# Gathering expert tiles six ahead of the scatter instead of five in an RWKV and mixture-of-experts layer

## The reference

```python
xt = x.reshape(-1, Hv)
logits = xt @ wg
probs = jax.nn.softmax(logits, axis=-1)
idx = jnp.argmax(probs, axis=-1)
gate = jnp.take_along_axis(probs, idx[:, None], axis=1)
onehot = jax.nn.one_hot(idx, Ev, dtype=x.dtype)
expert_out = jnp.einsum('nh,eoh->neo', xt, W) + b[None, :, :]
combine = onehot * gate
out = jnp.einsum('ne,neo->no', combine, expert_out)
...
x = _layernorm(x + out, axis=-1)
```

## Time and profile before

| | |
|---|---|
| median of 3 runs | 673.41 us (673.17 to 674.12) |
| the profiled execution's own time | 673.86 us |
| its span, first to last instruction | 671.9 us |
| busy share PE / DVE / ACT / POOL | 88% / 82% / 60% / 46% |
| the first gather starts | 510.99 us |
| the turn of tile 3 starts | 527.06 us |
| the turn of tile 38 starts | 649.60 us |
| the last scatter is issued | 662.83 us |

### The profile page before, as it was taken

The page is one execution under the profiler, slowest core; times in us unless marked ns, Lnnn a source line. Parts: engine busy times, 40 slices in busy tenths (PEclk is TensorE's granted clock), DMA queues, the critical chain, the costliest instruction groups (busy, mean ns, idle before and its releaser), DMA issues. The chain is left out here.

```text
span 671.9 us, 8986 instructions
## 1 busy us (share of the span) xinstructions
PE 588.4 (88%) x2484; PEld 437.8 (65%) x2485; DVE 554.0 (82%) x866; ACT 403.5 (60%) x735; POOL 306.2 (46%) x230
## 2 busy tenths in 40 slices
PE   0676789999999999999999999999754999999992
PEld 0464666677768667668768767865554777776771
DVE  7959898998999999999999899679956666766761
ACT  3356475477567665756747647666340577777773
POOL 4744544443551552454444544247404255655641
PEclk9779898999999999999999999999855899999997
DMA  8030020031022003004103103394203566777650
GB/s 311 4 125 1 0 63 0 2 109 63 17 72 86 32 32 125 31 0 156 31 0 126 62 1 110 98 383 161 60 20 112 139 210 217 228 218 223 222 166 6
DMA packets 36562, 67.60 MB, mean 101 GB/s; under 512 B 8560, under 2 KB 8560, under 8 KB 36532
## 3 DMA queue, kind: packets, MB, share of 16 engines
q1 hardware_dynamic: 30292, 48.29, 21.8%
q0 software_dynamic: 6240, 18.94, 9.1%
HBM read 50.17 MB, written 18.88 MB: 103 GB/s over the span
## 5 line engine op out<-in xcount | busy, mean ns | idle before, releaser
L980 POOL TENSOR_TENSOR mixed<-unsplit,mixed 128x1024 fp32r<-128x1024 f32 x44 | 104.5, 2396 | 133.8 <-ACT mixed L666 133.8
L447 PE MATMUL kb<-mixed,w_kvr 128*128 128x512 f32 x384 | 99.4, 410 | 23.5 <-DVE mixed L1321 16.5
L447 PE MATMUL vb<-mixed,w_kvr 128*128 128x512 f32 x384 | 104.1, 423 | 14.4 <-DVE evn L1159 9.0
L632 PE MATMUL y_ps<-w_e_hi,xgT 128*128 x312 | 108.6, 410 | 0.0
L447 PE MATMUL rb<-mixed,w_kvr 128*128 128x512 f32 x384 | 100.6, 411 | 4.6 <-DVE ee L1173 3.6
L447 PEld LDWEIGHTS kb<-mixed,w_kvr 128*128 128x128 f32 x384 | 74.4, 197 | 42.2 <-issue 16.2
L465 PE MATMUL y_ps<-w_o,rw 128*128 128x512 f32 x224 | 100.7, 592 | 0.0
L447 PEld LDWEIGHTS vb<-mixed,w_kvr 128*128 128x128 f32 x384 | 75.7, 201 | 36.5 <-DVE evn L1159 11.8
L447 PEld LDWEIGHTS rb<-mixed,w_kvr 128*128 128x128 f32 x384 | 72.5, 191 | 26.1 <-issue 6.2
L1110 DVE SCALAR_TENSOR_TENSOR unsplit<-diff,vec,xb 128x512 f32<-128x512 f32 x96 | 74.2, 834 | 8.1 <-PE kb L447 6.2
L990 POOL TENSOR_TENSOR ee<-ee,state 128x512 f32<-128x512 f32 x32 | 35.0, 1093 | 94.3 <-DVE state L1143 93.6
(11 more groups left out here) (198 smaller groups left out, 1052.0 us busy)
## 6 DMA issues: line engine op xcount, KB each, us to landing
bias<-b_experts SPq DMA_DIRECT2D x39, 256.0 KB
w_e_raw<-w_experts SPq DMA_DIRECT2D x8, 1024.0 KB, 11.7
rows<-x SPq DMA_DIRECT2D x28, 256.0 KB, 2.6
x_rows<-rows SPq DMA_DIRECT2D x28, 256.0 KB, 2.1
xb<-xT SPq DMA_DIRECT2D x4, 1026.0 KB, 5.5
xb<-xT SPq DMA_DIRECT2D x3, 1024.0 KB, 5.2
w_raw<-w_square SPq DMA_DIRECT2D x2, 1024.0 KB, 10.0
xb<-xT SPq DMA_DIRECT2D x2, 512.0 KB, 5.0
```

The source lines that it names most:

```text
L447: mm = pe.matmul(bank, w_kvr[m][:, a, h, o:o + P], mixed[m][:, bb, h, :], start=(k == 0), stop=(k == 3 * CH - 1))
L632: mm = pe.matmul(y_ps[:, parity, :], xgT[:, third, a, c, :], w[:, bass.ds(e, 1), c, :].rearrange("p u o -> p (u o)"), start=(c == 0 and (a ...
L980: pool.tensor_tensor(mixed[m][:, LO, 2 * hp:2 * hp + 2, :], unsplit[m][:, LO, 2 * hp:2 * hp + 2, :], mixed[m][:, HI, 2 * hp:2 * hp + 2, :] ...
```

## The change

The constant `AHEAD` = 5 is gone. GpSimd issues `RING` = 6 gathers first, and in the loop g(k + 6) ahead of S(k). The waits of each gather and scatter are the same as before, and so are their numbers, 39 each.

```diff
 RING = 6
 PART = 8
 BIAS_RING = 3
-AHEAD = 5
 POOL_EXPERTS = 5
...
-            for k in range(AHEAD):
+            for k in range(RING):
                 gather(k)
             for k in range(SORTED):
-                if k + AHEAD < SORTED:
-                    gather(k + AHEAD)
+                if k + RING < SORTED:
+                    gather(k + RING)
                 scatter(k)
```

## The result

| | before | after |
|---|---|---|
| median of 5 runs | 673.41 us (672.1 to 674.12) | 664.29 us (663.91 to 665.15) |
| the profiled execution's own time | 673.86 us | 664.29 us |
| its span | 671.9 us | 662.2 us |
| T(3) | 527.06 us | 526.96 us |
| T(38) | 649.60 us | 639.96 us |

The ratio is 0.9868 with a 95% interval of 0.9853 to 0.9883: 1.3% faster. The forecast was 664.2 us in a range of 663.1 to 667.5. The span lost 9.7 us, and T(38) moved by 649.60 - 639.96 = 9.64; T(3) before it moved by 0.1 and the stretch from T(38) to S(38) by 0.01 (13.22 us). The whole difference in these two executions thus lies between T(3) and T(38). That the median came out within 0.1 us of the forecast is partly luck: in another execution of the changed kernel, shown further down, T(3) falls 2.4 us earlier.

A forecast was written before the change was run, and what follows sets the result against it. PE was taken to set the pace, waiting for gathers that land late. Removing 9.49 us of loss, less 0.1 for GpSimd's lag, takes 673.86 to 664.5 (664.0 from the median); forecast 664.2 us, range 663.1 to 667.5.

The forecast's parts named there:

- The loop over three tiles: Turn, expert, normalisation, scatter, gather, turn span three tiles, leaving a gather 3.94 us to land; it needs 3.9 at best.
- the clean pace: PE's step per tile without a wait, read from T(8) to T(12): 3.23 us, against 3.50 from T(3) to T(38).
- The gain of 9.49 us: Expert stage, T(3) to T(38): 122.54 us against 113.05 at 3.23 us a tile; no turn waits for a gather any more.
- The wait of the gather, 0: On GpSimd, g(k + 6) waits for add(k) ahead of S(k); that wait has been over for 1.6 us, costing 0.
- The upper bound, a gap of 0.9 us instead of 0.3: Slow rival: GpSimd gathers still waiting cost 0.9 us of gap, a step of 3.82 us, 680.1 us in all; chance 0.06.
- GpSimd's own pace, 0.1 of 0 to 1: GpSimd's step of 3.20 to 3.28 us barely keeps up, lagging 1.6 us by S(32); 0.1 us lost, range 0 to 1.
- The DMA engines, 0: Same bytes in less time raise the DMA share from 0.72 to 0.78; crowded landings may grow, but cost 0.
- the allowance of 7.17 us: Time from a gather's start to its turn on PE after the change, against the largest landing seen, 5.72 us.
- The second rival, later landings: Crowded gather landings grow by a third, 5.7 to 7.6 us; 3 us come back, giving 667.2 us; chance 0.09.
- The first rival, the landing is not what PE waits for: Something that comes with the gathers holds PE, so nothing is gained: 673.4 us as a median; chance 0.06.
- The rule on a DMA's time: About 2.0 us plus bytes over 436 GB/s gives 2.6 us per gather; by it the change would bring nothing.
- The end: S(38) follows T(38) by 13.23 us, with only the last experts and no gathers; this stays.

The follow-up runs named there:

- four ahead: The kernel before with four gathers issued first and g(k + 4) ahead of S(k): 717.61 us, ratio 1.0639.
- without bias traffic: The kernel before, five gathers ahead, loading only partition 0 of the bias row from tile 3 on: 665.79 us, ratio 0.9877 to the kernel before.
- warm start with five ahead: The kernel before with 18 matmuls added on PE before T(0): 670.54 us, ratio 0.9962.
- the kernel with one scatter earlier: The changed kernel with g(0) to g(6) first, then g(k + 7) ahead of S(k): 664.16 us, ratio 0.9861 to the kernel before.
- the warm start added: The changed kernel with 18 matmuls added on PE before T(0): 661.42 us, ratio 0.9819 to the kernel before.
- six ahead when the gathers were held back until an add: The changed kernel with g(k + 6) waiting for add(k + 1) instead of add(k): 664.11 us, ratio 0.9866 to the kernel before.

## Why the prediction was right, step by step

- **The loop over three tiles.** Right in kind: four ahead gave 6.4% more, six ahead a stage free of waits. One number in it was mis-sized. I read T(12) - g(12) = 3.91 us as a quiet landing, and concluded that the loop "closes with nothing to spare" at 3.94. T(12) showed no wait, so 3.91 was only an upper bound. With four ahead two turns that do wait show 3.31 and 3.51, and without bias traffic the median is 3.4. Against such a landing the allowance of 3.94 leaves about 0.5 us to spare, and the kernel before lost its 9.5 us to crowded landings alone: without the bias loads, nothing was lost with five ahead. The sum did not depend on it, since it was made from the clean pace.
- **The gain of 9.49 us.** 122.54 - 113.00 = 9.54 us, read from T(3) to T(38). The 3.1 us of it that no wait names were rightly counted in: with six ahead the unnamed long steps are gone too, and without the bias traffic all but two small ones. In the warm start with five ahead, whose trace tells every landing, several turns for which the profile names no wait start just 0.12 us after their gather landed, T(19) and T(34) among them, with steps of 3.33 and 3.31 us.
- **The wait of the gather, 0.** Right: only g(6) waits. The upper bound, a gap of 0.9 us instead of 0.3, was wrong in itself. The 0.9 in front of a scatter goes with its wait for yo(k): S(11) starts 570.01 - 569.18 = 0.83 us after the end of yo(11), and so does nearly every scatter of both kernels up to S(33), within 0.04 us. When yo(k) is long done the gap is 0.30, as the kernel with one scatter earlier shows; and there a gather follows the add that it waits for after 0.28 us.
- **GpSimd's own pace, 0.1 of 0 to 1.** The term is 0, for the same reason. I took 1.01 + 0.30 + gather + 0.91 for the shortest step, but the 0.91 is not GpSimd's own. With all waits over, the parts seen add up to 1.01 + 0.30 + 0.97 + 0.30 = 2.58 us; that is an estimate, since no run had such a step. The lag of 1.6 us by S(32) did not come: S(32) is 4.45 us behind T(35), where I had allowed for up to 6.0.
- **The DMA engines, 0.** The cost was 0 and the share 0.78, but the reason given was wrong. I argued that a gather "meets the same neighbours" and so lands as before. The median landing is 5.3 us in the changed kernel, in both of its profiles, and 4.0 with five ahead and the full traffic (the warm-start kernel with five ahead; the list of the kernel before gives none). What made the term 0 was the allowance of 7.17 us alone. The second rival, later landings, was right that they grow, and by about a third in the median. It was wrong at the top: it needed 7.6 us, and the largest landing in the view of the changed kernel's first profile is 6.1, so it had no price.
- **The first rival, the landing is not what PE waits for.** Wrong, as four ahead and five ahead without the bias traffic show. But one reason that I gave against it was a wrong reading: the gaps from gather to turn do not lie at 5.0 to 5.7 us "only where PE waited". T(8) started 5.79 us after g(8) without a wait, because T(7) had been late, and T(16) waited and started only 4.34 us after g(16).
- **The rule on a DMA's time** (the Trainium skill, DMA: Bandwidth & Descriptors, Anatomy of one DMA) gave an estimate of 2.6 us for a gather. The median without bias traffic is 3.4 us, and 5.3 in the changed kernel. Measured landings decide here; the estimate is too low even for the smallest of them, 3.2 us with four ahead.
- **The end.** T(38) to S(38) was 13.22 us, forecast 13.23.

## What to carry to other kernels

When a ring of buffers is refilled from an engine that also waits for the result, write down how many tiles the loop spans, and compare (tiles x pace) minus the fixed part with the landing time. One place moved in the order gave a whole tile of lead here, 3.23 us, with the same buffers, because the refill needed only the last read of the slot and not the store behind it. More lead than the latest landing needs gave nothing. A landing time can be read from a turn only where the engine waited for it; anywhere else it is an upper bound.

## What the runs showed of the hardware

The same 39 gathers landed in 3.4 us in the median without the bias traffic, with five ahead and with six. With it they landed in 3.5 with four ahead, at a slower pace; in 4.0 with five ahead (the warm-start kernel); in 5.3 with six ahead, and 5.0 with the warm start added; and in 4.1 with seven and 4.2 with six ahead when the gathers were held back until an add. The pace alone does not explain the growth from five to six: in the kernel before the steps from T(8) to T(12) run at 3.23 us too, and T(12) had its gather after at most 3.91. Nor does the distance to the bias load: from the packet records of the traces the first packet of a bias load comes 1.0 us behind the first of a gather in the kernel before, and 0.9 us in the changed one (medians), while the gather's own packets spread over about 2 and about 3 us. What lengthens them stays open; no run varied it by itself, and it costs nothing here.

The step from T(2) to T(3), the first expert, took 6.0 us in two executions (527.06 - 521.08 before, 526.96 - 520.96 after), 4.6 in another of the changed kernel (524.61 - 520.00) and 3.25 with PE kept busy (523.56 - 520.31). Its length follows the moment at which the granted clock rises from 0.50 to 1.00: between 526 and 528 us in the changed kernel's first profile, between 522 and 524 in its second. Differences of 1.4 us between executions of one kernel come from there. Others arise earlier still: T(0) is at 518.37 and 517.41 in these two profiles of the changed kernel, and at 521.01 in the one with five ahead and little bias traffic, whose first gather starts 3 us later than in the kernel before (514.05 against 510.99). This is why small differences were read from T(3) on and not from medians.
